# Attention's maxima issued along a precomputed stream, at eight places of a step, with the second chunk first in unit 0

## The reference, cut to what matters

```python
D_MODEL, D_C, D_R, NH = (256, 128, 32, 16)      # head dimension 16
c_kv = x @ W_kv_down
k_rope = _rotary_apply(c_kv @ W_k_rope, cos, sin)
k = (c_kv @ W_k_up).reshape(Bb, Tt, NH, HD)
v = (c_kv @ W_v_up).reshape(Bb, Tt, NH, HD)
q = (x @ W_q).reshape(Bb, Tt, NH, HD)
q_rope = _rotary_apply(x @ W_q_rope, cos, sin)
scores = jnp.einsum('bqhd,bkhd->bhqk', q, k)
scores = scores + jnp.einsum('bqr,bkr->bqk', q_rope, k_rope)[:, None]
scores = scores / math.sqrt(HD + D_R)
scores = jnp.where(causal[None, None], -jnp.inf, scores)
w = jax.nn.softmax(scores, axis=-1)
attn = jnp.einsum('bhqk,bkhd->bqhd', w, v).reshape(Bb, Tt, D_MODEL)
return attn @ W_o
```

## Time and profile before

| | us |
|---|---|
| median of 3 runs | 1874.16 (1873.39 to 1887.14) |
| the profiled execution | 1872.57 |
| its span in the profile | 1870.9 |

### The profile page before, as it was taken

One profiled execution on the slowest core, in us unless ns is written; L12 is line 12 of the kernel. 1 busy time (PEld: TensorE's weight loads), 2 busy tenths in 40 slices (PEclk: granted clock), 3 DMA queues, 4 the chain that ended last, 5 costly groups with the idle time before them and its releaser, 6 DMA issues. The chain is left out here.

```text
span 1870.9 us, 34665 instructions
## 1 busy us (share of the span) xinstructions
PE 1542.4 (82%) x13054; PEld 791.8 (42%) x13054; DVE 1154.4 (62%) x3208; ACT 897.7 (48%) x1272; POOL 361.9 (19%) x432
## 2 busy tenths in 40 slices
PE   7993689999999999999999995710599967888898
PEld 5440122333333333333333334410478844566776
DVE  3846779787796877878787404730256665311675
ACT  2330345666666666666665762410367743311353
POOL 2461880000000000000000002237211100430011
PEclk9995799999999999999999997965799979999899
DMA  8288430402204040140401014412677710487001
GB/s 292 107 243 187 135 131 32 84 5 61 47 28 84 15 80 18 41 71 27 84 1 51 17 39 150 169 52 107 89 83 87 91 23 0 173 287 267 23 35 45
DMA packets 102198, 166.59 MB, mean 89 GB/s; under 512 B 23596, under 2 KB 72492, under 8 KB 100884
## 3 DMA queue, kind: packets, MB, share of 16 engines
q1 hardware_dynamic: 83124, 113.15, 25.5%
q0 software_dynamic: 16112, 47.59, 8.1%
q10 hardware_dynamic: 2800, 3.64, 0.5%
HBM read 107.76 MB, written 56.47 MB: 88 GB/s over the span
## 5 line engine op out<-in xcount | busy, mean ns | idle before, releaser
L909 ACT ACTIVATE at_pr<-ps 128x1024 f32<-128x1024 f32 (+3 forms) x640 | 546.8, 894 | 347.5 <-PE ps L849 218.4
L942 DVE TENSOR_REDUCE at_mx<-ps 128x1 f32<-128x512 f32 x768 | 489.0, 685 | 143.9 <-PE ps L801 135.6
L939 DVE CUSTOM_DVE_ANT_0 at_seen<-ps,later 128x384 bf16<-128x384 f32 (+3 forms) x512 | 229.2, 486 | 16.1 <-issue 10.7
L849 PE MATMUL ps<-bq,bk 64*128 64x512 f16 (+3 forms) x1280 | 223.8, 346 | 0.0
L846 PE MATMUL ps<-sqk 64*128 64x512 f16 (+3 forms) x1280 | 171.8, 347 | 11.4 <-DMA sqk<-at_mr 11.4
L846 PE MATMUL ps<-at_sqk 64*128 64x512 f16 (+3 forms) x1280 | 171.2, 346 | 6.2 <-DMA at_sqk<-at_mr 5.5
L801 PE MATMUL ps<-sqk 64*128 64x512 f16 (+3 forms) x640 | 120.7, 374 | 59.9 <-DVE at_mx L942 29.5
L825 PE MATMUL ps<-at_pr,vl 128*32 128x512 f32 (+3 forms) x1280 | 150.5, 542 | 0.0
L825 PE MATMUL ps<-at_pr,at_vl 128*32 128x512 f32 (+3 forms) x1280 | 150.0, 541 | 0.1
L801 PE MATMUL ps<-at_sqk 64*128 64x512 f16 (+3 forms) x640 | 114.7, 355 | 20.1 <-DVE at_mx L942 8.1
L801 PEld LDWEIGHTS ps<-sqk 64*128 64x128 f16 x640 | 31.1, 94 | 207.9 <-DVE at_mx L942 123.7
(11 more groups left out here) (277 smaller groups left out, 2358.2 us busy)
## 6 DMA issues: line engine op xcount, KB each, us to landing
mi_tz<-d_z SPq DMA_DIRECT2D x32, 1024.0 KB, 7.2
ex_xr<-d_rows SPq DMA_DIRECT2D x39, 256.0 KB
d_rows<-at_nil POOLq DMA_DIRECT2D x31, 322.0 KB
d_va<-st_va SPq DMA_DIRECT2D x8, 1024.0 KB, 4.3
d_o<-at_oc POOLq DMA_DIRECT2D x32, 256.0 KB, 2.3
at_pw<-in_w POOLq DMA_DIRECT2D x24, 256.0 KB, 3.3
d_w<-at_ph POOLq DMA_DIRECT2D x24, 256.0 KB, 2.4
exw<-d_w SPq DMA_DIRECT2D x8, 768.0 KB, 13.4
```

What stands on the lines that cost most here:

```text
L849: ins = pe.matmul(ps[:, 2 * f + r, off:CH], g.bk[half[r], b, k], g.bq[half[r], b, q], start=False, stop=t < 0)
L909: act.activation(pr[:, n % 2, f, :, off:CH], ps[:, 2 * f:2 * f + 2, off:CH], ACT.Exp, scale=INV_SCALE).then_inc(exp_done[f], 1)
L939: ins = dve.tensor_tensor_reduce(seen[:, turn, r, 0:n], src, g.later[:, CH - n:CH], 1.0, LOWEST, ALU.add, ALU.max, dst)
L942: ins = dve.tensor_reduce(dst, src, AX.X, ALU.max)
```

## The change

Units and steps stay, with these changes:

- **Order.** Unit 0 works through its chunks as 2, 3, 1, 0. The other units keep 3, 2, 1, 0.
- **Stream.** All pairs of all units form one list: the pairs of a chunk, its turn, then the next chunk. Each chunk now has its own turn (4 in a unit instead of 2), its own shift (4 DMAs, so 16 in a unit) and its own semaphore. The maxima may run ahead as far as the next unit's first two chunks, from step 6 on (`HEAD_STEP`, `AHEAD`).
- **Places.** A step has eight places: 0 before it, 1 to 6 behind each of the six products of scores (behind the mask where there is one), 7 behind the weighted values.
- **Walk.** `schedule()` walks through the steps with a clock for TensorE (`now`) and one for VectorE (`free`, `first_done`), in ns, and puts the next pair or turn at the first place at which it could begin by then, with 60 ns of allowance, at place 6 with 500. Before a chunk's first step it puts all that is left of that chunk's pairs and its turn, waits until `FETCH` (5000 ns) behind the turn, and puts pairs into that time.
- **SyncE.** The order is: the unit's first shift, the next unit's load, its other three shifts.
- **VectorE.** Ahead of a diagonal pair it waits for the pair that last used the same buffer, no more for the pair just before.

The diff, cut:

```diff
-def attn_steps():
-
-    return [(qc, kb) for qc in reversed(range(NCH)) for kb in range(TPC * (qc + 1))]
-
-
-def max_pairs():
-
-    return [(i, qc * TPC + t, j) for qc in reversed(range(NCH)) for t in range(TPC) for i in range(2)
-            for j in range(qc + 1)]
+def attn_steps(chunks):
+
+    return [(qc, kb) for qc in chunks for kb in range(TPC * (qc + 1))]
+
+
+def max_pairs(chunks):
+
+    return [(i, qc * TPC + t, j) for qc in chunks for t in range(TPC) for i in range(2) for j in range(qc + 1)]
...
-    REST_END = 9
-    FIRST_END = 13
-    M0, FIRST_M0, M_END = REST_END + 2, FIRST_END + 2, 37
...
+    NU = NG * NB
+    OPENING, FALLING = [2, 3, 1, 0], [3, 2, 1, 0]
+    ORDER = [OPENING] + [FALLING] * (NU - 1)
+    STEPS = [attn_steps(o) for o in ORDER]
+    PAIRS = [max_pairs(o) for o in ORDER]
+    ENDS = [{qc: n for n, (qc, kb) in enumerate(st)} for st in STEPS]
+    NS, NPAIR = len(STEPS[0]), len(PAIRS[0])
...
+    def pair_slot(v, k):
+        return 2 * k + max(m for m in range(NCH) if upto(v, m) <= k)
...
+    HEAD_STEP, AHEAD, FETCH, SLACK = 6, 2, 5000, 500
+
+    def ticks(w):
+        return w * 0.4167
+
+    def reduce_time(v, k):
+        return width(v, k) / 0.96 + (76 if diagonal(v, k) else 70)
+
+    def schedule():
+
+        stream = []
+        for v in range(NU):
+            for m in range(NCH):
+                stream += chunk_pairs(v, m) + [("turn", v, m)]
+        todo, at = {}, 0
+        now = free = first_done = last_ready = 0.0
+        turned_at = {}
+
+        def may(u, s):
+            if at == len(stream):
+                return False
+            kind, v, n = stream[at]
+            return v <= u or (v == u + 1 and s >= HEAD_STEP and n < (AHEAD if kind == "turn" else upto(v, AHEAD)))
+
+        def begin_of(x):
+            return last_ready + 350 if x[0] == "turn" else first_done + 60
+
+        def issue(place):
+            nonlocal at, now, free, first_done, last_ready
+            x = stream[at]
+            todo.setdefault(place, []).append(x)
+            at += 1
+            now = max(now, begin_of(x))
+            if x[0] == "turn":
+                now += 64
+                free = first_done = last_ready = max(free, now + 400) + 200
+                turned_at[x[1], x[2]] = free
+            else:
+                now += ticks(width(*x[1:])) + 10
+                start = max(free, now + 430 - ticks(width(*x[1:])))
+                first_done = start + reduce_time(*x[1:]) + 80
+                free = start + 2 * reduce_time(*x[1:])
+                last_ready = free + 80
+
+        for u in range(NU):
+            for s in range(NS):
+                qc, kb = STEPS[u][s]
+                t = kb - TPC * qc
+                w = CH - max(t, 0) * P
+                if kb == 0:
+                    m = ORDER[u].index(qc)
+                    while (u, m) not in turned_at:
+                        issue((u, s, 0))
+                    ready = turned_at[u, m] + FETCH
+                    while may(u, s) and max(now, begin_of(stream[at])) + 300 < ready:
+                        issue((u, s, 0))
+                    now = max(now, ready)
+                for i in range(1, 8):
+                    now += ticks(4 * w) + 200 if i == 7 else ticks(w) + (106 if t >= 0 and i % 3 == 0 else 0)
+                    while may(u, s) and begin_of(stream[at]) <= now + (SLACK if i == 6 else 60):
+                        issue((u, s, i))
+        return todo
+
+    TODO = schedule()
...
+            for m in range(NCH):
+                shift(0, m)
+            for u in range(1, NU):
+                shift(u, 0)
+                if u + 1 < NU:
+                    load(*divmod(u + 1, NB))
+                for m in range(1, NCH):
+                    shift(u, m)
...
+            def ahead(u, s, place):
+                for kind, v, n in TODO.get((u, s, place), []):
+                    if kind == "turn":
+                        turn_maxima(v, n)
+                        continue
+                    if v and n == 0:
+                        if v == 1:
+                            pe.wait_ge(once, 16 * N_ROPE_LOADS)
+                        pe.wait_ge(ld[v % NB], loaded(*divmod(v, NB)))
+                    maxima(v, n)
...
+                        ahead(u, n, 3 * f + part + 1)
...
+                    ahead(u, n, 3 * f + 3)
 
                 for s in range(NS):
-                    if first and s == chunk_end[3] + 1:
-                        pe.wait_ge(shift_ld[0], 192)
-                    if not first and s == chunk_end[2] + 1:
-                        pe.wait_ge(shift_ld[b], grp * 128 + (128 if b else 192))
-                    if s == (FIRST_M0 if first else M0) and not last:
-                        if first:
-                            pe.wait_ge(once, 16 * N_ROPE_LOADS)
-                        pe.wait_ge(ld[nxt[1]], loaded(*nxt))
-                    own, ahead = pairs_of(s, first, last)
-                    todo = [(u * UNIT, rest_slot(first, p), b, p) for p in own] + \
-                        [((u + 1) * UNIT, 2 * p, nxt[1], p) for p in ahead]
-                    n0, n1, _ = places(len(todo))
+                    ahead(u, s, 0)
+                    if STEPS[u][s][1] == 0:
+                        pe.wait_ge(shift_ld[b][ORDER[u].index(STEPS[u][s][0])], 64 * (grp + 1))
                     scores(s, 0)
-                    for x in todo[:n0]:
-                        maxima(*x)
                     scores(s, 1)
-                    for x in todo[n0:n0 + n1]:
-                        maxima(*x)
-                    if s == 0 and not first:
+                    if s == 0 and u:
                         weighted(*before, NS - 1)
                     if s >= 1:
                         weighted(grp, b, s - 1)
-                    for x in todo[n0 + n1:]:
-                        maxima(*x)
-                    if s == (FIRST_END if first else REST_END):
-                        turn_maxima(2 * u + 1, rest_slot(first, NPAIR), b)
-                    if s == M_END and not last:
-                        turn_maxima(2 * u + 2, 2 * N_MAIN, nxt[1])
+                    ahead(u, s, 7)
...
-                if p in DIAG:
-                    if not (isinstance(base, int) and base + slot == 0):
-                        dve.wait_ge(mx_done, base + (slot - 1))
-                    dve.memset(gap[:, :], 0.0)
...
+                if diagonal(v, k):
+                    if len(seen_at) >= 2:
+                        dve.wait_ge(mx_done, seen_at[-2])
+                        dve.memset(gap[:, :], 0.0)
+                    seen_at.append(v * UNIT + slot + 2)
...
+            def turn_maxima(v, m):
+
+                b, qc, slot = v % NB, ORDER[v][m], turn_slot(v, m)
+                dve.wait_ge(mx_done, v * UNIT + slot)
+                dve.tensor_reduce(mm[:, b, 32 * qc:32 * qc + HG * TPC].rearrange("p (h t) -> p h t", h=HG),
+                                  mx[:, :, qc * TPC:(qc + 1) * TPC, 0:qc + 1], AX.X, ALU.max).then_inc(mm_ready, 1)
+                rows = slice(32 * qc, 32 * qc + HG * TPC)
+                dve.wait_ge(mt_ready, NCH * v + m + 1)
                 dve.tensor_scalar(mr[rows, b, :], ps[rows, MAXB + slot % RING, 0:P], -1.0 / SHIFT_UNIT, None, ALU.mult)\
-                   .then_inc(mx_done, slots)
-
-            for p in range(N_PRE):
-                pair(0, 0, 2 * p, p)
-            final(0, 2 * N_PRE, 0, [3])
-            negate(0, 2 * N_PRE, 2, 0, slice(0, 32))
+                   .then_inc(mx_done, turned(v, m) - (v * UNIT + slot))
...
+                    for place in range(8):
+                        ahead(TODO.get((u, s, place), []))
```

More of the change, by code:

```diff
@@ new lines, in attn_steps, with upto, turn_slot, turned @@
+def attn_steps(chunks):
+    return [(qc, kb) for qc in chunks for kb in range(TPC * (qc + 1))]
+def max_pairs(chunks):
+    return [(i, qc * TPC + t, j) for qc in chunks for t in range(TPC) for i in range(2) for j in range(qc + 1)]
+def phase_attention(nc, g):
+    NU = NG * NB
[5 more added lines that the diff above has]
+    NS, NPAIR = len(STEPS[0]), len(PAIRS[0])
+    RING = 3
+    UNIT = 2 * NPAIR + NCH + 1
+    INV_STEP = 24
+    def upto(v, m):
+        return sum(2 * TPC * (qc + 1) for qc in ORDER[v][:m])
+    def pair_slot(v, k):
+        return 2 * k + max(m for m in range(NCH) if upto(v, m) <= k)
+    def turn_slot(v, m):
+        return 2 * upto(v, m + 1) + m
+    def turned(v, m):
+        return v * UNIT + (turn_slot(v, m) + 1 if m + 1 < NCH else UNIT)
+    def width(v, k):
+        _, qb, j = PAIRS[v][k]
+        return min(CH, (qb + 1) * P - j * CH)
+    def diagonal(v, k):
+        _, qb, j = PAIRS[v][k]
+        return j == qb // TPC
+    def chunk_pairs(v, m, n0=0, n1=None):
+        k0, k1 = upto(v, m), upto(v, m + 1)
+        return [("pair", v, k) for k in range(k0 + n0, k1 if n1 is None else k0 + n1)]
+    HEAD_STEP, AHEAD, FETCH, SLACK = 6, 2, 5000, 500
[53 more added lines that the diff above has]
+    TODO = schedule()
```

(28 more changed lines are left out.)

131 lines of the change are left out of this document (31 added, 100 removed).

## The result

The changed kernel takes 1853.24 us (median of 4 runs, 1848.04 to 1856.73), the one before 1875.81 beside it (4 runs, 1873.39 to 1887.14). The ratio is 0.9857, with a 95% interval of 0.9825 to 0.9889: 1.4% faster, within the range and 5 us above the predicted 1848. The profiled execution is the slowest of the four, 1856.73, with a span of 1854.9.

What follows compares the result with a forecast made beforehand. Bound by TensorE's stream and the VectorE reduces it feeds, with 8.4 us of waits per unit. Unit 1's start -23.2, six units -5.4, last unit +2.9: together -25.7, giving 1848 us; range 1820 to 1876.

Steps and rivals of the forecast that it cites:

- The opening comes back: Unit 0's start: chunk 2 first saves 11.2 us, about 8 of which return as a stall before chunk 3.
- The rest of unit 0: Unit 0 from chunk 3's first score: 28 steps, 52 pairs, turns, waits and half clock, 76.0 us, ending at 317.6.
- The border: Between units: 3.6 us waiting for shift rows (4.5 from turn to scores less 0.9) plus 1.1 for half clock.
- The clock: TensorE at half clock behind a border: 2.0 us lost, half taken (1.1); all seven borders falling would add 6 us.
- The waits inside: Units 1 to 6, within the steps: 2.2 us of waits per unit, bounds 1.0 to 4.0.
- The last unit: Attention's last unit takes over the lag, 44 pairs: 99.6 us instead of 96.7.
- Attention in sum: Unit 1's start -23.2, six units of 111.8 us -5.4, last unit +2.9: together -25.7 us.
- The total: Whole kernel: 1846.9 us in the profiled execution, 1848 us as median of the runs.
- Rival 1: Unit borders: the stream keeps up, 2 to 3 pairs decide, no wait; 1815 us, half of it 1832; chance 0.22.
- Rival 2: Unit borders grow to 9.0 us as next unit's chunk 3 isn't done; slower, 1878 us; chance 0.1.
- Rival 3: Units' steps don't improve: waits inside stay near 4 us; 13 us more, 1861 us; chance 0.15.
- Rival 4: Nothing changes: the opening's 11 us return wholly at chunk 3, unit 0 keeps its waits; 1874 us; chance 0.05.

Runs made afterwards that it cites:

- e1: The changed kernel with unit 0 in the old chunk order 3, 2, 1, 0: 1842.48 us, ratio 0.9844 to the kernel before.
- e5: The changed kernel once more, unaltered but for a blank line: 1846.03 us, ratio 0.985 to the kernel before.
- e3: The changed kernel with 4 of a unit's 80 pairs of maxima left out: 1808.12 us, ratio 0.9649 to the kernel before.
- e8: A repeat of e1, the changed kernel with unit 0 in order 3, 2, 1, 0: 1841.36 us, ratio 0.9835 to the kernel before.
- e2: The changed kernel with a wait of 560 ns instead of 500 allowed at place 6: 1833.85 us, ratio 0.978 to the kernel before.
- e6: The changed kernel with e1's order, 560 ns at place 6, 120 at other places, and traced durations in the walk (fetch 4300 ns): 1824.23 us, ratio 0.9738.
- e7: The changed kernel with 60 ns instead of 500 allowed at place 6: 1898.68 us, ratio 1.0138 to the kernel before.
- e4: The changed kernel with pairs only at places 3, 6 and 7 instead of all eight: 1870.56 us, ratio 0.9968 to the kernel before.
- e9: e6 with 60 instead of 120 ns of allowance at the places, run on another chip: 1856.84 us, ratio 0.983 to the kernel before.

## Why the prediction was right, point by point

**The opening comes back: right, nearly to the number.** First score at 195.3, measured 196.10 with a first pair that began 0.7 later (156.48 against 155.76). Chunk 3's first score at 241.6, measured 241.75, with three pairs and a turn ahead of it where four were forecast. That this is 0.15 off is in part luck: chunk 2's steps ended at 231.97 instead of 230.2, 1.8 later, and the stall behind them took 9.8 instead of 11.4. e1 shows the consequence, which the forecast gave as 8 of 11 us and the runs as all of it: 10.7 saved, 11.4 given back in unit 0 as a whole, since the old order, in the new stream, has no such stall.

**The rest of unit 0: right.** 76.0 us, measured 76.15 (241.75 to 317.9). 

**The border: right in kind, mis-sized, and held by something else.** The count of pairs held: 77 to 78 in the steps and four at the border were forecast, 77 and three came. Forecast were 3.6 us of waiting for the shift rows plus 1.1 for the clock. Measured are gaps of 2.52 to 2.69 at all seven, and TensorE at its lower level for about 3.4 us behind four of them. What failed is the term "4.5 from turn to scores less 0.9": the turn stands 3.1 us before the unit's end (314.80 to 317.9), not 0.9, so most of the fetch is over when the border begins. The gap is there because the walk takes 5000 ns for the fetch and fills them with pairs, and the last pair's wait of 0.79 holds the score. The rows were there at 318.95, 3.5 us behind the negation's end (315.47) and 1.5 before 320.44. That a shorter `FETCH` alone would bring that 1.5 was not tried apart.

**The clock: right to count, priced too high.** Units with the lower clock at their start last 111.5 to 111.7, those without 110.7 and 110.8: 0.8 us each, not 2.0. The stage table shows the same four at 0.98. It goes with the clock and not with the unit: unit 4 lasts 111.5 here with a fall and 110.8 in e1 without, unit 2 110.8 here without and 111.7 in e5 with one. Four of seven fell, where the forecast had half. If all seven had fallen, it would have been 2.5 us more than measured. The warning of the Trainium skill (TensorE: Matmul & The Clock Gate, Why this matters for your kernels) against idle gaps between bursts of matmuls agrees with the trace in the direction.

**The waits inside: mis-sized the other way.** 89.0 + 14.5 + 1.4 = 104.9 is the stream without waits. A unit at full clock lasts 110.7, of which the border's idle time is 2.0 (the gap of 2.5 less the columns of its three pairs): 3.8 are left inside, near the upper bound of 4.0, where 2.2 were forecast and 8.4 less the border's 1.2 had been before, 7.2. The waits that the rows show there are 3.3 us, at place 6 (1.4, as at 391.05) and behind the weighted values (1.8). Border and inside together are 6.4 with the clock (111.3 - 104.9), against 6.9 forecast; hence 111.3 a unit instead of 111.8.

**The last unit: exact.** 99.6, measured 99.53. Nothing new took VectorE's or ScalarE's or SyncE's time, as costed: VectorE 91.35 of 111.

**Attention in sum:** 30.7 us gained, 25.7 forecast. Of the 5.0 more, 1.9 are unit 1's start (320.44 instead of 322.3, with the first pair 0.7 later) and 3.0 the six units.

**The total: right, in part by luck.** The sum took everything outside attention as unchanged. In the profiled execution it was 14.8 us longer, in the medians 30.7 - 22.6 = 8.1, in e5's comparison 30.4 - 27.5 = 2.9. Attention's gain beyond the forecast and this loss point opposite ways, and that the total came within 5 us is in part luck. Of the 14.8, 9.7 are TensorE's matmuls taking longer, with 23 us more at the lower level of its clock; the rest are waits: those for `ex_xr` and `mi_tz` grew by 7.0, some others fell a little. That the change itself causes this is not shown: e3, e8 and e1, built from it, have later stages no more than 1.4 us longer than before's, or shorter, and by the medians of e5 and e8 next to nothing is left. The traces differ by some 20 us behind attention, which the range should name when a forecast rests on one execution. What sets the clock there stays open.

**The rivals.** Rival 1 (borders closed, 2 to 3 pairs decide): did not happen, and e2, e3 and e6 show that it was one small constant or four pairs away. Its price was too high: with all borders closed e2 takes 1833.85, not 1815, for the waits inside grew with it (5.4 us a unit where 2.2 were taken). That this is near the 1832 worked out for half of it is chance. Rival 2 (borders grow, slower) did not happen either; e7 shows it, and e4 up to next to no change. Rival 3 had 4 us of waits inside a unit, and 3.8 came: on this term it was closer than the forecast, and only the shorter border kept its 1861 away. Rival 4: true of the opening, not of the unit.

## What to carry to other kernels

Where one engine's fine-grained feeding of another decides, count how many feeds fit per step and how many are needed per round. Here, with the balance within a few per cent, a constant of 60 ns decides between no border at all and one at each unit, and one of 440 ns between faster and slower. Allowing a short wait now was cheaper than a place later (e2 against the changed kernel, e6 against e9), since what doesn't fit waits at the border with nothing beside it. Work moved ahead of a start comes back as a stall unless the stream behind it has room: look for the place where it falls due.

## What the runs showed of the hardware

- Behind borders of 2.5 us, filled in part by three pairs of small matmuls, TensorE's clock went to its lower level (1.2 GHz) in four cases of seven (at 320.6, 542.5, 655.1 and 877.0), for about 3.4 us, at a cost of 0.8 us of the unit. The same borders gave four of seven in e1, e5 and e8 each; borders of 2.07 us (e3) none of three, of 3.4 to 3.6 us with four pairs (e9) seven of seven. Units 1 to 6 of e2 and e6, with closed borders, ran at 1.00 throughout. The earlier trace rows had it after an idle time of 2.01 and not after 1.15.
- At the lower level a full pair alone takes 1.40 us from one to the next, at the higher 1.20 (233.23 to 234.43). Halving TensorE's rate costs such a chain a sixth; in both, each pair waits 0.8 us for VectorE's reduce.
- Identical later stages took between 745.8 and 767.2 us from one build and execution to the next (775.5 on another chip), with the clock at its lower level for 179.8 to 207.1 us of them and waits for the same DMAs (`ex_xr`) of 8.0, 9.2 and 13.0 us in before, e5 and after. The kernel before took 1889 us on another chip and 1874 to 1877 on the others.
